# Attention and cosine-grouped normalisation on one core: the gram step moved ahead of the next values, and the sums of squares taken from its diagonal

## What is computed

```python
x_f = einsum('oc,bcn->bon', Wf, xf) + bf    # 16 channels
x_g = einsum('oc,bcn->bon', Wg, xf) + bg    # 16 channels
x_h = einsum('oc,bcn->bon', Wh, xf) + bh    # 128 channels: the "values"
beta = softmax(einsum('bci,bcj->bij', x_f, x_g), axis=-1)
y = x + gamma * einsum('bci,bij->bcj', x_h, beta)
...
y_n = y / max(norm(y, axis=pixels), 1e-12)
cos = einsum('bcn,bdn->cd', y_n, y_n) / B
_, idx = top_k(-abs(cos).T, 4)              # each channel's 4 least alike channels
gs, gsq = sums of y and of y*y over the pixels, added over those channels
out = g * (y - mean) * rsqrt(var + eps) + b # mean and var from gs and gsq
```

## Time and profile before

| what | us |
|---|---|
| median of 3 runs | 207.89 (207.61, 207.89, 321.08) |
| the profiled execution | 206.57 |
| its span | 204.8 |
| PE busy in the span | 179.0 |
| DVE, ACT, POOL busy | 157.9, 155.9, 122.6 |

### The profile page before, as it was taken

One profiled execution on the slowest core, in us unless ns is written; L12 is line 12 of the kernel. 1 busy time (PEld: TensorE's weight loads), 2 busy tenths in 40 slices (PEclk: granted clock), 3 DMA queues, 4 the chain that ended last, 5 costly groups with the idle time before them and its releaser, 6 DMA issues.

```text
span 204.8 us, 2724 instructions
## 1 busy us (share of the span) xinstructions
PE 179.0 (87%) x775; PEld 123.5 (60%) x775; DVE 157.9 (77%) x395; ACT 155.9 (76%) x256; POOL 122.6 (60%) x106
## 2 busy tenths in 40 slices
PE   7849999999999999999999999999999989973100
PEld 2525655577867776787678667867686667541000
DVE  1798887787989688968896889788987986456650
ACT  2365478889999999989998999899989979240420
POOL 4000004936978797879787987799679966510400
PEclk9999999999999999999999999999999999995555
DMA  5891100020002000200010001100110000000298
GB/s 201 317 360 32 26 3 2 0 53 0 0 3 51 0 0 2 54 2 2 0 32 19 3 0 26 27 3 2 26 26 0 0 3 0 0 0 2 84 402 334
DMA packets 4014, 10.72 MB, mean 52 GB/s; under 512 B 544, under 2 KB 672, under 8 KB 4000
## 3 DMA queue, kind: packets, MB, share of 16 engines
q1 hardware_dynamic: 3424, 9.18, 13.5%
q10 hardware_dynamic: 576, 1.38, 1.8%
HBM read 4.52 MB, written 4.19 MB: 43 GB/s over the span
## 4 chain that ended last, share of the span: by engine, by line
PE 74%; DVE 10%; issue 6%; ACT 4%; POOL 2%; DVEq 0%; ACTq 0%; POOLq 0%
PE o_ps L645 41%; PE s_ps L626 12%; PE w_ps L612 6%; PE w_ps L607 5%; DVE nmax L413 3%; PE w_ps L660 3%; PE w_ps L654 3%; PE o_ps L604 2%; DVE xy L597 2%; ACT probs_high L336 1%; ACT probs L327 1%; DVE values L444 1%; DVE g_rows L433 1%; POOL v_low L287 1%; PE s_ps L654 1%
## 5 line engine op out<-in xcount | busy, mean ns | idle before, releaser
L266 POOL TENSOR_TENSOR probs_low<-probs,probs_high 128x1024 fp32r<-128x1024 f32 x40 | 95.7, 2392 | 55.0 <-ACT probs_high L336 55.0
L327 ACT ACTIVATE probs<-s_ps,nmax 128x1024 f32<-128x1024 f32 x64 | 71.2, 1112 | 20.6 <-DVE nmax L413 20.6
L413 DVE TENSOR_REDUCE nmax<-s_ps 128x1 f32<-128x1024 f32 x64 | 77.8, 1218 | 9.4 <-PE s_ps L626 9.1
L626 PE MATMUL s_ps<-g_rows,fg_parts 128*128 128x512 f32 x128 | 46.9, 450 | 2.9 <-ACT probs L327 2.3
L645 PE MATMUL o_ps<-probs,vnorm 128*128 128x512 f32 x96 | 45.2, 593 | 1.0 <-DVE vnorm L428 1.0
L336 ACT ACTIVATE probs_high<-probs 128x1024 fp32r<-128x1024 f32 x40 | 42.1, 1053 | 0.1
L645 PE MATMUL o_ps<-probs_high,v_high 128*128 128x512 f32 x80 | 35.0, 438 | 1.1 <-POOL v_low L287 1.1
L645 PE MATMUL o_ps<-probs_high,v_low 128*128 128x512 f32 x80 | 31.5, 394 | 0.0
L645 PE MATMUL o_ps<-probs_low,v_high 128*128 128x512 f32 x80 | 31.3, 392 | 0.0
L626 PEld LDWEIGHTS s_ps<-g_rows,fg_parts 128*128 128x128 f32 x128 | 21.5, 190 | 12.4 <-issue 6.0
L645 PEld LDWEIGHTS o_ps<-probs,vnorm 128*128 128x128 f32 x96 | 18.0, 189 | 16.0 <-issue 12.5
(11 more groups left out here) (86 smaller groups left out, 171.9 us busy)
## 6 DMA issues: line engine op xcount, KB each, us to landing
xy<-x_dram SPq DMA_DIRECT2D x7, 512.0 KB, 6.3
out_dram<-xy SPq DMA_DIRECT2D x5, 512.0 KB, 5.8
g_rows<-fg_parts SPq DMA_DIRECT2D x14, 128.0 KB, 2.2
out_dram<-xy ACTq DMA_DIRECT2D x2, 512.0 KB, 4.1
xy<-x_dram SPq DMA_DIRECT2D x2, 256.0 KB, 3.6
out_dram<-xy SPq DMA_DIRECT2D x2, 256.0 KB, 2.2
wd<-wide_dram ACTq DMA_DIRECT2D x1, 256.0 KB, 4.2
wd<-wide_dram ACTq DMA_DIRECT2D x1, 66.5 KB, 3.5
```

Source lines behind the costliest of these rows:

```text
L266: nc.gpsimd.tensor_tensor(probs_low[i % PARTS][:, :], probs[n % PROBS][:, :], probs_high[i % PARTS][:, :].bitcast(F32), ALU.subtract).then ...
L327: nc.scalar.activation(probs[n % PROBS][:, :], s_ps[n % 2][:, :], ACT.Exp, bias=nmax[:, n % T:n % T + 1], accum_out=rsum[:, n % T:n % T + ...
L413: nc.vector.reduce_max(nmax[:, n % T:n % T + 1], s_ps[n % 2][:, :], AX_X, negate=True).then_inc(max_ready, 1)
L626: last = nc.tensor.matmul(s_ps[n % 2][:, h], fg_parts[b % 2][:, t * P:(t + 1) * P], g_rows[b % 2][:, h], start=True, stop=True)
```

## The change

The turned y, its two copies and its gram are moved ahead of the next image's values; the sum of squares of images 0 to 6 is no longer taken by ACT from y, but by DVE from the diagonal of the gram in PSUM. For that, POOL once builds `twice` [128 x 256], the identity beside twice the identity; DVE multiplies the 256 gram columns by it and accumulates, which is the sum over the pixels of high squared plus twice high times low. The square of the low part is left out of it. The norm is then one slot later on POOL. Both halves of the values now go through the second bank of `w_ps`, one after the other, and the turned gram stands in columns 256 to 383 of the first bank.

```diff
+            pool.wait_ge(const_in, 16)
+            nc.gpsimd.tensor_copy(twice[:, 0:P], ident).then_inc(twice_set, 1)
+            nc.gpsimd.tensor_scalar(twice[:, P:2 * P], ident, 2.0, None, ALU.mult).then_inc(twice_set, 1)
...
-                    if b > 0 and t == 3:
+                    if b > 0 and t == 4:
                         invert_norm(b - 1)
...
                     if t == 2 and b > 0:
-                        act.wait_ge(y_ready, H * b)
-                        nc.scalar.activation(squares[:, :], xy[:, b - 1, :], ACT.Square,
-                                             accum_out=stats[:, b - 1 + B:b + B]).then_inc(sq_ready, 1)
-                    if t == 4 and b > 0:
                         act.wait_ge(yT_made, b)
                         nc.scalar.activation(yT[:, :, 0:P], w_ps[:, :].rearrange("p (t c) -> p t c", c=P),
                                              ACT.Copy).then_inc(yT_high, 1)
...
+            def pick_squares(b):
+                dve.wait_ge(gram_made, b + 1)
+                dve.wait_ge(twice_set, 2)
+                nc.vector.scalar_tensor_tensor(picked[:, :], w_ps[:, 0:2 * P], 1.0, twice[:, :], ALU.mult, ALU.mult,
+                                               accum_out=stats[:, b + B:b + B + 1]).then_inc(sq_ready, 1)
...
                     if t == 1 and b < L:
                         make_parts(b + 1, 0)
+                    if t == 1 and 0 < b < L:
+                        make_parts(b + 1, 1)
                     if t == 2 and b == 0:
                         make_parts(1, 1)
-                    if t in (2, 3) and 0 < b < L:
-                        add_value_bias(b + 1, t - 2, w_ps)
...
-                    if t == 5 and b > 0:
+                    if t == 3 and b > 0:
                         dve.wait_ge(yT_high, b)
                         for h in range(H):
                             low_part(slice(h * TH, (h + 1) * TH), w_ps[:, halves[h]])
+                    if t == 4 and b > 0:
+                        pick_squares(b - 1)
+                    if t in (5, 6) and 0 < b < L:
+                        add_value_bias(b + 1, t - 5, w_ps[:, halves[1]])
                     if t == 6 and b > 0:
-                        scale_gram(b - 1, w_ps)
-                    if t == 7 and b > 0:
-                        add_gram(b - 1, w_ps[:, BANK:BANK + P])
+                        add_gram(b - 1, w_ps[:, 2 * P:3 * P])
...
-                    if t == 1 and 0 < b < L:
-                        make_parts(b + 1, 1)
...
+                    if t == 5 and b > 0:
+                        scale_gram(b - 1, w_ps)
...
                 if b < L:
-                    pe.wait_ge(v_ready, H * (b + 2))
+                    pe.wait_ge(parts_ready, H * (b + 2))
...
             def next_values(b, h):
-                pe.wait_ge(parts_ready, H * b + h + 1)
-                project_values(b, w_ps, h)
+
+                if b == 1:
+                    pe.wait_ge(parts_ready, H * b + h + 1)
+                elif h == 0:
+                    pe.wait_ge(yT_ready, H * (b - 1))
+                else:
+                    pe.wait_ge(v_ready, H * b + 1)
+                project_values(b, w_ps[:, halves[h if b == 1 else 1]], h)
...
-                    if t in (1, 2) and 0 < b < L:
-                        next_values(b + 1, t - 1)
+                    if t == 1 and b > 0:
+                        turn_y(b)
+                    if t == 3 and b > 0:
+                        pe.wait_ge(yT_ready, H * b)
+                        gram(w_ps, range(T)).then_inc(gram_made, 1)
                     if t in (2, 3) and b == 0:
                         next_values(1, t - 2)
-                    if t == 3 and b > 0:
-                        turn_y(b)
+                    if t in (4, 5) and 0 < b < L:
+                        next_values(b + 1, t - 4)
                     if t == 5 and b > 0:
-                        pe.wait_ge(yT_ready, H * b)
-                        gram(w_ps, range(T)).then_inc(gram_made, 1)
-                    if t == 6 and b > 0:
-                        turn_gram(b - 1, w_ps[:, BANK:BANK + P])
+                        turn_gram(b - 1, w_ps[:, 2 * P:3 * P])
```

More of the change, by code:

```diff
@@ L126, in build @@
         squares = sb("squares", [P, N])
+        twice = sb("twice", [P, 2 * P])
+        picked = sb("picked", [P, 2 * P])
         yT = sb("yT", [P, T, 2 * P], F32R)
@@ L166, in build @@
         zeros_set = sem("zeros_set")
+        twice_set = sem("twice_set")
         bias_ready = sem("bias_ready")
@@ L444, in add_value_bias @@
                 nc.vector.tensor_tensor(values[b % 2][:, h * TH:(h + 1) * TH, :],
-                                        source[:, halves[h]].rearrange("p (t c) -> p t c", c=P),
+                                        source.rearrange("p (t c) -> p t c", c=P),
                                         bias, ALU.add).then_inc(v_ready, 1)
@@ L482, in _ @@
             dve.wait_ge(const_in, 16)
-            add_value_bias(0, 0, o_ps)
+            add_value_bias(0, 0, o_ps[:, halves[0]])
             row_max(0)
-            add_value_bias(0, 1, o_ps)
+            add_value_bias(0, 1, o_ps[:, halves[1]])
             row_max(1)
@@ L502, in _ @@
                         make_parts(b + 1, 0)
+                    if t == 1 and 0 < b < L:
+                        make_parts(b + 1, 1)
                     if t == 2 and b == 0:
                         make_parts(1, 1)
-                    if t in (2, 3) and 0 < b < L:
-                        add_value_bias(b + 1, t - 2, w_ps)
                     if t in (3, 4) and b == 0:
-                        add_value_bias(1, t - 3, w_ps)
-                    if t == 5 and b > 0:
+                        add_value_bias(1, t - 3, w_ps[:, halves[t - 3]])
+                    if t == 3 and b > 0:
                         dve.wait_ge(yT_high, b)
@@ L611, in project_values @@
                 for t in range(h * TH, (h + 1) * TH):
-                    last = nc.tensor.matmul(to[:, t * P:(t + 1) * P], xy[:, b, t * P:(t + 1) * P],
+                    last = nc.tensor.matmul(to[:, (t % TH) * P:(t % TH + 1) * P], xy[:, b, t * P:(t + 1) * P],
                                             wd[:, WHT:WHT + P], start=True, stop=True)
@@ L675, in next_fg @@
                     pe.wait_ge(g_head, h + 1)
+                elif h == 1:
+                    pe.wait_ge(v_ready, H * b)
                 elif b == 2:
-                    pe.wait_ge(v_ready, H + h + 1)
-                elif h == 0:
-                    pe.wait_ge(gram_scaled, b - 2)
+                    pe.wait_ge(v_ready, H + 1)
                 else:
@@ L686, in turn_y @@
                 if b < L:
-                    pe.wait_ge(v_ready, H * (b + 2))
+                    pe.wait_ge(parts_ready, H * (b + 2))
                 else:
                     pe.wait_ge(gram_added, b)
+                    pe.wait_ge(v_ready, H * B)
                 transposes(xy[:, b - 1, :], w_ps, range(T)).then_inc(yT_made, 1)
             def next_values(b, h):
-                pe.wait_ge(parts_ready, H * b + h + 1)
-                project_values(b, w_ps, h)
+                if b == 1:
[5 more added lines that the diff above has]
+                project_values(b, w_ps[:, halves[h if b == 1 else 1]], h)
             pe.wait_ge(warm_set, 1)
@@ L703, in _ @@
             for h in range(H):
-                project_values(0, o_ps, h)
+                project_values(0, o_ps[:, halves[h]], h)
             pe.wait_ge(zeros_set, 2)
```

## The result

The changed kernel takes 209.37 us, the median of 6 runs (207.68 to 209.76); the kernel before, run beside it, 207.75. The ratio is 1.0079, 95% interval 1.0045 to 1.0113: slower by 0.8%, within the 2% of "no change", and near the forecast of 209.7. Two executions stand apart, one of the kernel before (321.08 us) and one of the run with the squares on ACT (211.34 us): they are in the medians and not in the ratios. The profiled execution of the changed kernel is also its fastest, 207.68 us with a span of 205.9 (before: 206.57 and 204.8). So it shows 1.1 us more, while the medians differ by 1.6.

What follows compares the result with a forecast made beforehand. PE's work was taken to bound images 1 to 6. Turned gram 1.55 plus POOL's norm 0.28 gave 1.83 us: 206.57 to 208.4 profiled, plus 1.3 for the median, 209.7 us (0.9% slower); range 207.3 to 211.5.

Steps and rivals of the forecast that it cites:

- PE waits for nobody: Kernel before, between 46 and 150 us: the time is PE's work, about 21.0 us an image, without waits.
- The turned gram's race: Images 1 to 5: PE's turned gram waits for DVE's scaled gram, 0.17 to 0.45 us each, taken as 0.31.
- gram 1.10: PE's new order, counted on image 5: the gram takes 1.10 us and ends at 132.36.
- POOL at the end of image 6: The norm, now between low parts of tiles 5 and 6, makes PE's products at 164.34 start 0.28 us later.
- Image 7 and the rest: Image 7, closing stretch, image 0 and stores: price 0; a missed 0.2 us margin costs at most 0.4 once.
- The pick at 0.45: DVE's new 256-column instruction from PSUM with accumulator: 0.45 us, bounds 0.35 and 0.84, cost to PE 0.
- PE's wait for low values: Start of image 7: PE waits about 0.9 us for POOL's low values; 0.66 us in the kernel before.
- Rival 1: Turned gram's wait is hidden; only POOL's 0.28 and up to 0.3 us remain: 208.2 us; chance 0.22.
- Rival 2: ACT's relief pays: PE's 0.66 us wait at 164.34 nearly goes, 0.58 us gained: 207.3 us; chance 0.12.
- Rival 3: Gram in slot 3 comes late, stalling PE 0.4 us in each of five images: 211.7 us; chance 0.10.
- rival 4: PE is not the bound; with ACT as bound, 6.8 us would go: 201.1 us; chance 0.02.
- rival 5: The change doesn't do what it says; the schedule differs from the order shown: 207.9 us; chance 0.02.

Runs made afterwards that it cites:

- the pick alone: Kernel before, order kept, ACT's squares of images 0 to 6 replaced by DVE's pick in slot 6, norm and scaled gram later: 219.65 us (before 207.38).

## Why the prediction was right, and where it was off

- **Bound by PE, pieces end to end.** Right as far as it went: who takes the squares doesn't matter (1.008 against 1.0079). "PE waits for nobody" was a misreading: the view of the waits from which it was taken has the gram's load wait five times for the low parts (1.5 us of PEld in all), and the gram's piece of the chain held a stall of 0.12 to 0.16 us an image.
- **The turned gram's race.** The step held: the place, the chain, images 1 to 5, and nearly one for one with DVE's length. "I take 0.31, the middle": 0.35 measured between the two kernels that differ only in it. Both ends of the race moved as counted: 2.84 us was DVE's side, and the trace has 138.97 - 136.15 = 2.82; PE's was 2.73, and the run with the gram scaled first has 139.50 - 136.75 = 2.75. An image was to take about 21.3 us and takes 21.2.
- **The term that was mis-sized** is "5 x 0.31 = 1.55": the net is 0.99. The race alone costs 5 x 0.35 = 1.75, more than forecast; the shorter gram gives back 0.12 to 0.16 us an image, 0.7 in all, and a remainder of under 0.1 isn't assigned. The step that was off is "gram 1.10", taken over unchanged into the count of the new order. The text counted 0.25 us to spare for the low parts and did not ask what that is worth. The runs with the low parts later show that it's this: with two passes in front the gram is back over 1.10 and the image at 21.14.
- **POOL at the end of image 6.** Forecast 0.28, measured 0.28 (20.48 to 20.76). (By its rows the norm takes 0.88 us, not 0.86; in the trace after it holds POOL for 0.83, from 156.39 to 157.22.) With the gram scaled first, image 6 is still at 20.72, so the image's own stall at the turned gram does hide behind POOL, as said.
- **Image 7 and the rest at 0.** Measured 0.08 for image 7. The closing stretch is 0.3 shorter, which wasn't foreseen (below).
- **The pick at 0.45.** Measured 0.42 and 0.08 for the read of the accumulator; cost to PE none. **DVE at 18.5 us** an image: 18.53. **ACT at 18.8**: 19.2, only 0.7 below before. The run with the squares on ACT has 19.9 to 20.0 in the new order, so the squares are worth 0.7 to 0.8 of busy time and not 1.14; why stays open.
- **PE's wait for low values of "about 0.9 us"** before image 7's first product: it stayed at 0.66. The prediction added the 0.28 to this wait. But the products of the tile before wait for POOL's low values too, at PEld, so this last wait is POOL's time for a tile (2.77 us from 162.89 to 165.66, and 2.76 before) less PE's work between, which is the same in both. The 0.28 lies ahead of it.
- **The sum.** 1.83 forecast; 0.99 + 0.28 + 0.08 = 1.35 from image 1 to the first residual in the traces, 1.1 between the spans, 1.6 between the medians. The race was put too low and the gram's gain left out, and the two miss in opposite directions; that the median came within 0.4 us of the forecast owes something to this and to the scatter between executions.
- **The rivals.** Rival 1 falls with the five waits at the turned gram. Rival 2 needed a norm that costs POOL nothing and a turned gram that waits for nobody; the norm stands in the chain of image 6, and the turned gram waits. Rival 3 falls by the waits, rival 4 by images of 21.2 us and by the run with the squares on ACT, rival 5 by the new lengths of the stages. The rule of the Trainium skill that was weighed there (Perfetto Trace Analysis, Identifying the Most-Contended Engine: headroom by MFU and the busy share of the weight loads, of which only the second is looked at here) doesn't hold for the length of an image here: PEld is busy 15.7 of 21.2 us, and still the delays of PE in images 1 to 5 showed in their length, while ACT's 0.7 us did not. The row of the weight loads is worth reading all the same: the stall that the forecast overlooked shows as 0.31 us of idle time at PEld before the gram's loads, and not at PE. Not every idle time there is a stall, as the turned y shows.

## What to carry to other kernels

Before taking over a piece's length into a new order, look at the weight loads inside it: the same eight products took 0.95, 1.07, 1.10 or 1.22 us, depending on how early the last writer of their weights was done. When a step is moved so that two engines race from one instruction, count both sides and put the consumer's producer ahead of whatever isn't due (here the two steps of the scaled gram ahead of a row maximum, which took the kernel back to the time of before). And a wait that goes away is worth only what the next longest chain leaves: 0.5 us won in image 6 came back as 0.7 in image 7.

## What the runs showed of the hardware

**The clock early in the run.** Executions of one kernel differ by about 2 us, once by 2.8 (the norm taken twice), and the traces show a place where such a difference arises. The same two windows (columns as in the earlier trace rows), in the changed kernel and in the one with the gram scaled first:

```profile
8.00:16.00 8.00, 4.29 (x13) 2.02 (x12) 7.38 (x16) 4.05 (x7) 0.00 (x0) 1.00 0.83 333
16.00:24.00 8.00, 8.00 (x30) 4.74 (x29) 6.31 (x14) 3.89 (x7) 0.00 (x0) 1.00 0.15 33
```

```profile
8.00:16.00 8.00, 5.19 (x14) 2.66 (x13) 7.53 (x15) 3.39 (x5) 0.00 (x0) 0.73 0.88 357
16.00:24.00 8.00, 8.00 (x20) 3.86 (x19) 4.46 (x10) 3.90 (x8) 0.00 (x0) 0.84 0.08 16
```

PE's program is the same in both there. In the first the granted clock is 1.00 throughout (2.4 GHz); in the second it is 0.50 (1.2 GHz) from 12 to 18 us, and image 1's whole product begins at 43.2 us instead of 40.95. In both PE stands idle for 2.1 us, until 12.04 and 12.50 us; in the second the clock falls at the end of that idle time. Seven of the nine profiled variants had such a dip, the kernels before and after in their profiles not. It comes before the code that differs, and its size (2.3 us in this trace) is that of the whole effect studied here, so totals of single profiles mislead: the kernel with the gram scaled first has a longer span (206.1) than the changed kernel (205.9), and shorter stages. What decides it stays open.

**The clock at the end.** The closing stretch was 25.1 us in the two traces of the old order (before, and the pick alone) and 24.7 to 24.9 in all nine of the new one. Between 185 and 187 us, before and after:

```profile
185.00:187.00 2.00, 1.06 (x3) 0.39 (x3) 1.12 (x7) 0.00 (x0) 0.00 (x0) 0.50 0.01 4
```

```profile
185.00:187.00 2.00, 0.77 (x5) 0.38 (x4) 0.98 (x5) 0.00 (x0) 0.56 (x1) 1.00 0.00 0
```

Before, the clock had fallen to 1.2 GHz when the last turned gram came (0.48 us); after, it was still 2.4 GHz and the same product took 0.34 us, as did the next. That is the 0.3 us. The other traces agree: this product takes 0.47 us in the pick alone, where the clock had fallen too, and 0.34 in all of the new order, where it falls only after it. In both kernels PE had been busy without a break in image 7 until its last product, and sparsely after it. Why the clock falls later in the new order stays open; each kernel has one trace.
